# Eight small re-orderings in a two-layer Mamba, attention and MLP kernel

## The reference

```
xn = x * rsqrt(mean_c(x^2) + 1e-6) * norm_w
mamba(s): u, z = split(in_proj_w @ s); u = silu(causal_conv4(u) + b)
          dt, Bm, Cm = split(x_proj_w @ u); delta = softplus(dt_proj_w @ dt + dt_b)
          h_t = exp(delta_t * A) * h_(t-1) + delta_t * u_t * Bm_t   (16 states, A = -exp(A_log))
          y_t = sum_n h_t[n] * Cm_t[n] + u_t * D;  out_proj_w @ (y * silu(z))
g   = (mamba(xn) + flip(mamba(flip(xn)))) * scale_mod
loc = sigmoid(depthwise3x3(xn) + dw_b) * xn
x   = x + res_scale * (g + loc)                     # layer 0
t   = x as tokens
t   = t + causal_attention(layernorm(t))            # 6 heads of 64, with biases
t   = t + kron(p1, p2) @ gelu(kron(c1, c2) @ layernorm(t))   # 384 -> 1536 -> 384
```

## Time and profile before

| | |
|---|---|
| median of 3 runs | 4171.29 us (4167.19 to 4175.09) |
| profiled execution, its own time | 4170.78 us |
| its span | 4169.0 us |
| mean granted TensorE clock | 0.879 |
| busy, share of the span | PE 81%, DVE 86%, ACT 61%, POOL 66% |
| depthwise convolution starts (L1166) | 47.80, 467.15, 949.65, 1430.98, 1911.38, 2392.85, 2875.46, 3355.14 us |

### The profile page before, as it was taken

The page is one execution under the profiler, slowest core; times in us unless marked ns, Lnnn a source line. Parts: engine busy times, 40 slices in busy tenths (PEclk is TensorE's granted clock), DMA queues, the critical chain, the costliest instruction groups (busy, mean ns, idle before and its releaser), DMA issues.

```text
span 4169.0 us, 39529 instructions
## 1 busy us (share of the span) xinstructions
PE 3387.6 (81%) x11610; PEld 1710.0 (41%) x11626; DVE 3590.0 (86%) x2721; ACT 2558.3 (61%) x3547; POOL 2760.9 (66%) x1692
## 2 busy tenths in 40 slices
PE   6503499978898798978899798988999788976997
PEld 2201145623374245623365234732356233741472
DVE  4999998999899998999989998999989998997121
ACT  3533557665675767756676656757567656755362
POOL 2988786676766777676866767667876767675000
PEclk9756699989999799988999899987999889987998
DMA  2999797887878898888978978787978889788000
GB/s 82 229 238 232 191 236 173 213 198 197 216 184 197 197 217 193 193 201 200 230 169 208 212 190 213 184 195 200 233 173 210 196 202 214 171 207 188 6 7 15
DMA packets 220548, 772.36 MB, mean 185 GB/s; under 512 B 24908, under 2 KB 40574, under 8 KB 220062
## 3 DMA queue, kind: packets, MB, share of 16 engines
q0 software_dynamic: 114048, 415.29, 51.6%
q1 hardware_dynamic: 106270, 354.32, 25.8%
HBM read 339.60 MB, written 39.85 MB: 91 GB/s over the span
## 4 chain that ended last, share of the span: by engine, by line
PE 43%; DVE 23%; issue 14%; ACT 9%; POOL 7%; DMA 3%; SPq 0%; ACTq 0%; DVEq 0%; POOLq 0%
DVE pB L1205 15%; PE pW L674 9%; PE pW L591 9%; PE pW L479 7%; POOL hb L1388 5%; DMA y<-hb 3%; PE pW L556 3%; PE pW L607 2%; PE pW L522 2%; PE pW L570 2%; ACT pt L1008 2%; PE pW L534 2%; POOL prob L1369 2%; PE pW L649 1%; DVE hb L1214 1%
## 5 line engine op out<-in xcount | busy, mean ns | idle before, releaser
L1205 DVE TENSOR_TENSOR_SCAN pB<-pB,hb 128x1024 f32<-128x1024 f32 x768 | 1756.8, 2288 | 22.6 <-ACT pB L830 15.6
L1403 POOL DMA_DIRECT2D y<-hb x768 | 730.0, 950 | 753.4 <-DVE hb L1214 699.1
L1388 POOL TENSOR_TENSOR hb<-du_f,b_row 128x1024 f32<-128x1024 f32 x384 | 1003.9, 2615 | 177.9 <-DVE du_f L1154 131.3
L1388 POOL TENSOR_TENSOR hb<-uc_b,b_row 128x1024 f32<-128x1024 f32 x384 | 1002.7, 2618 | 73.8 <-DMA y<-hb 55.8
L1214 DVE TENSOR_TENSOR hb<-pB,c_row 128x1024 f32<-128x1024 f32 x768 | 940.0, 1224 | 45.4 <-DVE pB L1205 1.4
L830 ACT ACTIVATE pB<-delta,vec 128x1024 f32<-128x1024 f32 x384 | 429.0, 1117 | 321.1 <-DVE hb L1214 321.0
L830 ACT ACTIVATE pB<-xres,vec 128x1024 f32<-128x1024 f32 x384 | 428.8, 1118 | 295.5 <-DVE hb L1214 294.4
L674 PE MATMUL pW<-area,pt 128*128 128x64 f32 x3456 | 435.2, 280 | 20.1 <-ACT pt L1008 12.5
L674 PEld LDWEIGHTS pW<-area,pt 128*128 128x128 f32 x3456 | 407.6, 194 | 69.9 <-ACT pt L1008 59.8
L1249 DVE TENSOR_REDUCE stat<-pW 128x1 f32<-128x640 f32 (+7 forms) x361 | 258.6, 752 | 162.2 <-PE pW L594 162.2
L498 PE MATMUL pW<-area,xn_area 128*128 128x512 f32 x576 | 270.7, 625 | 49.4 <-DVE area L1292 36.1
(11 more groups left out here) (172 smaller groups left out, 4979.5 us busy)
## 6 DMA issues: line engine op xcount, KB each, us to landing
y<-hb POOLq DMA_DIRECT2D x768, 512.0 KB, 7.0
b_row<-bc_rows SPq DMA_DIRECT2D x256, 512.0 KB, 5.7
c_row<-bc_rows SPq DMA_DIRECT2D x256, 512.0 KB, 5.2
du_f<-in_x SPq DMA_DIRECT2D x8, 1536.0 KB, 13.1
kept_residual<-in_x SPq DMA_DIRECT2D x8, 1536.0 KB, 18.7
xres<-kept_residual SPq DMA_DIRECT2D x8, 1536.0 KB, 14.8
out_x<-xa SPq DMA_DIRECT2D x8, 1536.0 KB, 7.6
kept_residual<-hb POOLq DMA_DIRECT2D x16, 512.0 KB, 5.3
```

The source lines that it names most:

```text
L1205: dve.tensor_tensor_scan(flow(d, buf), flow(d, buf), flow(d, hb[r % NHB][:, :]), 0.0, ALU.mult, ALU.add).then_inc(scan_done, 1)
L1388: pool.tensor_tensor(hb[r % NHB][:, :], du[d][:, k, :], b_row[g % 2][:, :], ALU.mult)\
L1403: pool.dma_start(y[:, k, :], hb[r % NHB][:, :], accum_op=ALU.add).then_inc(y_in[k], 16)
```

## The change

Eight edits, in the order of the diff:

1. Tap 8 of the depthwise branch is made after the last silu, not before the fifth. Two gates are computed, then the narrow copies, then the third gate.
2. `next_norm` goes from row 67 to row 68. The next sample's mean (`next_mean`) waits for all six `wo_add`, not four, since `wo` now writes its tiles to banks 2, 3, 0, 1, 2, 3.
3. The cast of the low MLP part goes from VectorE (inside `mlp_split`) to ScalarE (`mlp_low`); `mlp_split` runs a row earlier, its rest (`mlp_fix`) in row 74 as before.
4. `step_abs` goes ahead of the projections' items in rows 23, 26 and 29.
5. First loads: x first, then seven small constants (`first_in`), then w_in, then eight more (`consts_in`). Preparations are moved into functions: on ScalarE and TensorE behind the squares and the mean of sample 0, on VectorE behind its norm; the splitting of the MLP weights goes behind sample 0's depthwise convolution.
6. The tiles of the out projection, of `ctx_t`, `wo`, `wo_add` and of the query projection go by halves: all three channel tiles of the first token half, then of the second. Waits follow: a mean of a half waits for three tiles, `wo` for as many evacuated tiles as it needs.
7. In iteration 8 (`alone`) Ln and Exp of the layer norms run for each half by itself, and the query projection and `mlp_in` begin with a finished half.
8. VectorE's first row comes ahead of the third sum of the softplus and its product.

```diff
-TAPS = (0, 3, 4, 6, 7, 9, 9)
+TAPS = (0, 3, 4, 6, 7, 8, 8)
...
-    ... ("next_rstd", 0, S1 + 5), ("next_norm", 0, S1 + 6)]
+    ... ("next_rstd", 0, S1 + 5), ("next_norm", 0, S1 + 7)]
-    + [("mlp_in", 0, S1 + 11), ("mlp_cast", 0, S1 + 12), ("mlp_split", 0, S1 + 13)] + ...
+    + [("mlp_in", 0, S1 + 11), ("mlp_cast", 0, S1 + 12), ("mlp_split", 0, S1 + 12),
+       ("mlp_low", 0, S1 + 13), ("mlp_fix", 0, S1 + 13)] + ...
+SOON = [x for x in BEHIND if x[0] == "step_abs"]
+SLOTS = [[... for kind, n, row in STEPS + FINISH + SOON + PLAN + [x for x in BEHIND if x not in SOON] if row == r]
...
+        def proj_bank(b, n):
+            return pW[:, (n + 2) % 4 if alone(b) else n % 2, :]
+        def proj_tile(n):
+            return (n % KT, n // KT) if n < 6 else ((n - 14) // 2, n % 2)
...
@@ sync: w_in behind x and the seven constants of first_in @@
-        NCONST = 16 * 15
+        NFIRST, NCONST = 16 * 7, 16 * 8
...
@@ out_project, ctx_t, wo (TensorE), finish, wo_add (VectorE), ctx_t (ScalarE) @@
-                    m, c = t // 2, t % 2
+                    m, c = t % KT, t // KT
...
@@ ln_mean, on TensorE @@
-                            pe.wait_ge(wo_add, at(6, a, 6))
+                            pe.wait_ge(wo_add, at(6, a, 3 * c + 3))
@@ proj @@
-                    pe.wait_ge(ln_xn, at(4, a, 2))
+                    pe.wait_ge(ln_xn, at(4, a, 1 if n < (KT if alone(b) else 1) else 2))
@@ wo @@
-                    pe.wait_ge(ct_evac, at(6, a, 6))
-                    if n >= 4:
+                    if n < 4:
+                        pe.wait_ge(ct_evac, at(6, a, n + 3))
+                    else:
                         pe.wait_ge(wo_add, at(6, a, n - 3))
-                    project(pW[:, n % 4, :], o_w, ...
+                    project(out_bank(n), o_w, ...
@@ mlp_in @@
-                    pe.wait_ge(ln_xn, at(4, a, 4))
                     for c in range(2):
+                        pe.wait_ge(ln_xn, at(4, a, 3 + c))
@@ next_mean @@
-                    pe.wait_ge(wo_add, at(6, b - 1, 4))
+                    pe.wait_ge(wo_add, at(6, b - 1, 6))
...
@@ ScalarE @@
+                    for bank, c in [(pW[:, 0, :], 1), (pW[:, 1, :], 2)] if alone(b) else [(pS, 2)]:
+                        (wait for the variance of half c, Ln, Exp of that bank)
+                elif kind == "mlp_low" and early:
+                    act.wait_ge(xr_step, at(5, a, 2))
+                    act.copy(xr_b, xr_rest[:, :]).then_inc(xr_step, 1)
...
-                    gates(b)
+                    tap_row_of(b, TAPS[6], 9)
+                    gates(b, 0, 2)
                     narrow_copies(b, 0)
+                    gates(b, 2, 3)
...
@@ VectorE @@
-                    dve.wait_ge(xr_step, at(5, a, 2))
-                    dve.tensor_copy(xr_b, xr_rest[:, :]).then_inc(xr_step, 1)
+                elif kind == "mlp_fix" and not early:
...
-                    for k in range(KT):
+                    for k in range(2):
                         soft_sum(b, 0, k)
                         times_u(b, k)
                     for r, d, n, k in rows():
                         ...
                         scan_row(b, r, n, k, d)
                         output_row(b, r, n, k, d)
+                        if r == 0:
+                            soft_sum(b, 0, 2)
+                            times_u(b, 2)
```

More of the change, by code:

```diff
@@ L339, in load_next @@
                 sp.dma_start(xnext, x[b].rearrange("(k p) t -> p k t", p=128)).then_inc(xn_in, 16)
-            sp.dma_start(ip_w, w_in.rearrange("(k p) e -> p k e", p=128)).then_inc(win_in, 16)
             load_next(0)
@@ L769, in iteration @@
                         step_size(b, 0, k)
+                    if isinstance(b, int) and b == 0:
+                        pe.wait_ge(fc_split, 5)
                     if layer1:
@@ L866, in silu_z, with gates @@
                     act.activation(zs[:, m, :], zs[:, m, :], ACT.Silu).then_inc(zs_ready, 1)
-            def gates(b):
-                for k in BRANCH:
+            def gates(b, lo, hi):
+                for k in BRANCH[lo:hi]:
                     if k < VK:
@@ L969, in item @@
                 elif kind == "ln_rs" and not early:
-                    act.wait_ge(ln_var, at(4, a, 2 * n + 2))
-                    act.activation(pS, pS, ACT.Ln, bias=eps5).then_inc(ln_log, 1)
-                    act.wait_ge(ln_log, at(2, a, n + 1))
-                    act.activation(pS, pS, ACT.Exp, scale=-0.5).then_inc(ln_rs, 1)
+                    for bank, c in [(pW[:, 0, :], 1), (pW[:, 1, :], 2)] if alone(b) else [(pS, 2)]:
+                        inc = 1 if alone(b) else 2
+                        act.wait_ge(ln_var, at(4, a, 2 * n + c))
+                        act.activation(bank, bank, ACT.Ln, bias=eps5).then_inc(ln_log, inc)
+                        act.wait_ge(ln_log, at(4, a, 2 * n + c))
+                        act.activation(bank, bank, ACT.Exp, scale=-0.5).then_inc(ln_rs, inc)
                 elif (kind, n) == ("proj", 17) and early:
@@ L1071, in iteration @@
                             copy_u(0, t)
+                        act.wait_ge(prep_dve, 2)
                     for i in range(6):
@@ L1083, in iteration @@
                         soft_log(b, 0, k)
+                    if isinstance(b, int) and b == 0:
+                        act.wait_ge(fc_split, 5)
                     for k in range(2):
@@ L1121, in _ @@
-            dve.wait_ge(prep_pe, 1)
-            for k in range(KT):
-                dve.tensor_scalar(kin_w[:, k, :].rearrange("p (q i) -> p q i", q=4),
-                                  early[:, 160 + KI * k:192 + KI * k].unsqueeze(1).broadcast_to([128, 4, KI]),
-                                  pW[:, 0, k:k + 1], None, ALU.mult)
-            dve.tensor_tensor(kout_w, prob[0:KI, 0:C], pW[0:KI, 1, 0:C], ALU.mult)
-            dve.tensor_copy(small[:, 8:10], pW[:, 2, 0:2]).then_inc(prep_dve, 1)
@@ new lines, in prepare @@
+            def prepare():
+                dve.wait_ge(prep_act, 2)
+                dve.tensor_scalar(vec[:, :, V_A:V_A + NS], vec[:, :, V_A:V_A + NS], -1.0, None, ALU.mult)
+                dve.tensor_scalar(bq_s, vec[:, :, V_BQ], 0.125, None, ALU.mult)
+                dve.wait_ge(prep_pe, 1)
+                for k in range(KT):
+                    dve.tensor_scalar(kin_w[:, k, :].rearrange("p (q i) -> p q i", q=4),
+                                      early[:, 160 + KI * k:192 + KI * k].unsqueeze(1).broadcast_to([128, 4, KI]),
+                                      pW[:, 0, k:k + 1], None, ALU.mult)
+                dve.tensor_tensor(kout_w, pt[0:KI, 0:C], pW[0:KI, 1, 0:C], ALU.mult)
+                dve.tensor_copy(small[:, 8:10], pW[:, 0, 8:10]).then_inc(prep_dve, 1)
+                dve.wait_ge(prep_dve, 1)
+                dve.tensor_copy(rs_col, small[:, 9:10])
+                dve.tensor_tensor(g_col, small[:, 8:9], small[:, 9:10], ALU.mult).then_inc(prep_dve, 1)
+                dve.wait_ge(prep_dve, 2)
```

117 lines of the change are left out of this document (63 added, 54 removed).

## The result

The changed kernel takes 4111.64 us (median of 4 runs, 4108.54 to 4115.67) against 4173.19 us for the kernel before on the same chip: a ratio of 0.9855, 95% interval 0.9838 to 0.9872. That is 61.6 us faster. The forecast was 4087, with a range of 4052 to 4120: the time lies inside the range, 25 us above the forecast; the change brings about three quarters of the 84 us that were forecast.

What follows compares the result with a forecast made beforehand. VectorE was taken to set the pace of all eight samples, with one chain through all engines before and after. Savings of 22, 1.3, 35, 35, 21 and 11.6 us less 42 lost give 83.9: 4087 us, range 4052 to 4120.

Steps and rivals of the forecast that it cites:

- The start: First loads reordered, x first and squares waiting for x alone: sample 0's mean starts 22 us earlier (20.4 to 23.8).
- The two softplus edits with the scan ahead: Waits before both directions' softplus sums shrink or go, with row 0's scan before the third: 35 us each, samples 1 to 7.
- the 5.0 of the sum: First direction, samples 1 to 7: row 1's scan starts 5.0 us earlier relative to the sample's start.
- The tail: Last norms by halves, after the last out projection: first MLP product earlier, 11.6 us saved (8 to 13).
- rival 2: MLP rows: VectorE's subtraction waits for GpSimd's multiply in place of the cast; 15.8 us less saved, 4103; chance 0.10.
- the cast gone, its subtraction still 1.21 us: MLP low part cast by ScalarE, hidden in row 74: VectorE saves 2.95 us in each of 7 samples, 21 us.
- The stall in row 68: Later next-sample mean delays rstd and row 68's decay; VectorE's scan waits 7.2 us; 42 us lost over samples 1 to 6.
- rival 1: The moved mean does not stall the rows, and the idle before the norm goes too: 4036; chance 0.12.
- 25 if TensorE keeps the upper level: Lower bound of the loss from moving the next norm, samples 1 to 6: 25 us if TensorE's clock stays high.
- Sample 0 has no wo_adds to wait for, and loses nothing: Moving the next norm a row on costs sample 0 nothing, against 7.0 us in each of samples 1 to 6.
- Rivals 3 and 4: 3 (0.04): row 68's chain grows, 4183 at 15 us a sample; 4 (0.02): TensorE absorbs the new order, 4178.
- abs and exp ahead: Second direction's abs and exp before the projections' evacuations: 5.0 us in each of samples 1 to 7, 35 us (24 to 46).

## Why the prediction was right, and where its sizes were off

**Right.** VectorE's idle time in the samples was the thing to count, and the change pays by it. The start (22 forecast, 21.3 measured) went as told, though x landed at 7.3 us on the clock where 8.6 were taken, and TensorE's mean took 8.3 us from idle. The two softplus edits with the scan ahead were forecast at 70 us together; undone one by one they cost 49, 21 and 0. In the change's own trace, samples 1 to 7, row 1 starts 3.5 to 5.0 us earlier, 4.3 in the mean, against the 5.0 of the sum, and rows 26 to 60 take 5.2 us less against 5.0: 66 us together, before what row 6 takes back. At the boundary itself the rows came out as forecast (the projection 5.36 us, the copies 22.1 us into the sample against 22.2, the sums' waits 1.1 us). The tail, from sample 7's last product of y and the gate (VectorE, starting at 3797.3) to the end, takes 314.5 us instead of 326.1: the 11.6 of the forecast. That it agrees to the tenth is luck: the first query tiles take 15.7 us instead of 17.75, which the forecast did not count, and the other kernels with norms by halves take up to 2.9 us less for this stretch.

**The cast, rival 2 (20 us too much).** The step that failed is "the cast gone, its subtraction still 1.21 us", 21 us for it. Rival 2, which the prediction gave 0.10, happened, and in a stronger form: it kept 5 us of gain, the cast on either engine shows none. The prediction argued that the subtraction starts 0.5 us after the row's output and GpSimd's multiply 1.0 us after it, so the subtraction would be first. It does start first by the records, 0.43 us ahead of the multiply, and waits nonetheless until the multiply has ended. The order of the starts in the records therefore does not decide who gets through. What the runs show for the MLP's rows is a count: with two or more VectorE operations behind a row's output (cast and copy; copy and subtraction; subtraction and copy) the second has waited, and with one none does. How early the operation starts fits as well: those that got through there start 0.88 to 1.00 us ahead of the multiply's record, those that waited 0.43 us ahead of it or less, and no run separates the two readings. Outside these rows neither is a rule. In row 68 of the change the norm's first product stands behind short fills of borders, starts 0.45 us ahead of the multiply, and gets through in all of samples 1 to 6:

```profile
811.99 1.21 DVE L1329 SCALAR_TENSOR_TENSOR area<-du_f,vec,prob 128x1024 f32<-128x1024 f32 x1
```

In the kernel before one such product (at 2752.76 us) started 0.53 us ahead of it and took 4.27 us. What decides within that half microsecond stays open. The Trainium skill (SBUF — State Buffer, "SBUF: two separate sides") has the two engines exclude each other for a whole instruction, VectorE's side being an operation in a two-port mode or with two SBUF inputs. The copy of 2.70 us against 0.42 and the subtraction of 4.16 against 1.21 agree with that; that whichever starts first has the pair does not fit the records' 0.43 us, unless the records' starts are not the moments at which the pair is taken, which no run here shows.

**The stall in row 68 (9 us too much loss in samples 1 to 6).** The chain was right link by link, wo_adds, mean, rstd, decay, scan, and rival 1 (no stall) is out. Its size was not: 7.0 a sample were forecast. The wait measures 5.67 us in most samples; counted as the sum counts it, from row 67 to row 72, it is +4.7 to +6.6, 5.5 in the mean, 33 us in place of 42. The mis-sized term is TensorE's mean, 7.1 us taken from a projection that follows 3.41 us of idle time, 5.41 measured at full clock behind 2.55; sample 5, with 3.81 us of idle time and 7.11 us, is the forecast's own case, with the forecast's wait (7.34 against 7.2). Undoing the edit gives 25 us, the prediction's own lower bound ("25 if TensorE keeps the upper level"), but partly by luck: some 3 of them are sample 0's, where nothing was forecast, and later rows give back part of the others.

**Row 6 (some 10 us not foreseen).** No step of the prediction names SP's queue at the boundary. Bringing the rows 4.5 us nearer to the projection also brought row 6's scan nearer to the B row of the third state, and that row is queued behind a weight load that waits for the out projection. By it samples 2, 3, 5, 6 and 7 gave back 1.4 to 2.2 us at row 6, 9.8 us together. Why the landing took 11.4 us where it had taken 5.6 in the same order of loads is not shown; the load moved behind the rows is worth 13 us. The forecast asked whether row 2's input would be in time, and not about the next states' loads.

**Sample 0 (8.0 us).** Forecast 1.3 us gained, measured 6.7 lost. The rows that slipped are row 5 (+2.5), rows 6 to 27 (+2.7 together, 1.9 of them at row 27), and row 71 (+3.0), where a decay stood behind ScalarE's evacuation of a tile that TensorE had not done:

```profile
363.72 0.59 ACT L933 COPY area<-pW 128x512 f32<-128x512 f32 x1 [2.07 <-PE pW L511]
364.20 2.16 ACT L850 ACTIVATE pB<-xres,vec 128x1024 f32<-128x1024 f32 x2
...
365.36 2.30 DVE L1243 TENSOR_TENSOR_SCAN pB<-pB,hb 128x1024 f32<-128x1024 f32 x1 [2.88 <-ACT pB L850]
```

The experiments that leave this sample as it is tell how firm that is: sample 0 lost 3.0, 3.8, 4.2, 4.4, 4.4, 5.5 and 5.7 us in them, 6.7 in the change's own profile. Two edits make it up. In every one of these profiles rows 68 to 71 lose 1.6 to 3.2 us net, and 0.5 or nothing with the norm back at its row; and at row 27 they are 2 to 3.5 us late where the scan goes first, and on time (-0.2 to +0.1) where the third softplus does, though the scan first gains 1.5 us at row 1. With both edits undone sample 0 takes 419.1 us, as before the change (419.3). "Sample 0 has no wo_adds to wait for, and loses nothing" failed: with the norm a row on the next projection starts later, and row 71 needs it. Why the scan first costs this sample some 3 us and the later ones nothing I have only argued (GpSimd gets du of tile 2 later and issues its rows in a burst); no run isolates it.

**The balance.** 57.3 measured in the spans against 83.6: sample 0 8.0, samples 1 to 6 14.2, sample 7 1.7, the stretch to the end 1.7 (zs waits 7.39 us for y where it waited 5.68), the start 0.7. In samples 1 to 6 the cast's 17.7, row 6's 7.6 and 5.2 of row 1's gain are missing, 30.5 us; the stall is 8.7 smaller than forecast, rows 7 to 60 bring 2.6 more, and the rows behind 76, of which the forecast said nothing, some 5. In sample 7 the cast and row 6 are lost, and 3.1 us are gained in rows 80 to 95. What gained there is open. So the forecast came as near as it did because its errors partly cancel. Rivals 3 and 4 are out: the chain in row 68 costs 5.5 and not 15, and abs and exp ahead were worth 49 us, not absorbed. For the wait of row 68 the prediction had named less than 3 us or more than 10 as its sign of being wrong; it is 5.6 to 7.3.

## What to carry to other kernels

A step moved earlier moves its consumers nearer to every later load: for the rows behind it, look at the queue of transfers as well as at the engines, and at what those loads stand behind. Before an operation is taken off an engine that shares time with another, look at what its neighbour in the row does when the slot is free: here the long form was a wait that passed to the next operation, and only with a single such operation left in the row was it gone. And price each part of a change with the others in place: the scan ahead was worth 0 us with one late load, and 13 us in the kernel without it.

## What the runs showed of the hardware

- VectorE and GpSimd: the second of two short VectorE operations behind a row's output took 4.16 us (subtraction, 1.21 alone), 2.70 or 3.22 us (bf16 copy on 32 partitions, 0.42 alone), beside a GpSimd multiply of 2.64 us, even where its record starts 0.43 us before that multiply's. A product of the norm that started 0.45 us before it took 1.21.
- TensorE kept the full granted clock behind 2.41 to 2.63 us of idle time ahead of the mean (12 products in 5.41 us, five samples); behind 3.81 us they took 7.11 at 0.76, and a stretch that follows 8.15 us of idle time was at 0.74, partly at the lower level (12 products in 7.28 us). The earlier trace rows had 7.12 us behind 3.41. The length of the idle time does not decide alone: in the kernel with the norm back at row 67 the next projection's 12 products took 7.12 us at 0.77 behind 1.95 us (at 3177.18 us).
- A row load of 512 KB took 11.4 us to land when issued 0.4 us behind a 576 KB weight load on the same queue, with a DMA share of 0.98 until then, and 5.6 us in the same order before the change, at 1.02; ahead of the weight load it took 5.4 us, at 0.84.
